# Latent attention with post-norm and a linear layer on one core: rotary parts sent through DRAM, first tables made on chip, output terms and pair order changed

## The reference

```python
HID, H, QLR, KVLR, DN, DR, DV = 512, 16, 384, 128, 128, 64, 128
cos, sin = rope_tables(s, DR)
cq = rms_norm(x @ w_qa.T, q_a_ln_w)                      # s x 384
q = (cq @ w_qb.T).reshape(b, s, H, DN + DR)
q_nope, q_pe = q[..., :DN], q[..., DN:]
q_pe = q_pe * cos + rotate_half(q_pe) * sin
ckv = x @ w_kva.T
k_pe = rotated(ckv[..., KVLR:])                          # one for all heads
kv = (rms_norm(ckv[..., :KVLR], kv_a_ln_w) @ w_kvb.T).reshape(b, s, H, DN + DV)
scores = (q_nope . k_nope + q_pe . k_pe) * (DN + DR) ** -0.5, causal
out = softmax(scores) @ v
x = layernorm(x + out @ w_o.T)
x = layernorm(x + x @ (weight * scale_weight[:, None]).T + bias)
```

## Time and profile before

| | us |
|---|---|
| median of 3 runs (lowest, highest) | 1889.14 (1888.12, 1890.75) |
| the profiled execution, its own time | 1888.21 |
| its span in the trace | 1886.5 |
| prepare phase, to TensorE's first instruction of attention | 176.4 |
| linear phase, from TensorE's first instruction | 1792.9 to 1886.5 |
| TensorE busy, share of the span | 1725.7, 91% |
| mean granted TensorE clock, share of full | 0.974 |

### The profile page before, as it was taken

One profiled execution on the slowest core, in us unless ns is written; L12 is line 12 of the kernel. 1 busy time (PEld: TensorE's weight loads), 2 busy tenths in 40 slices (PEclk: granted clock), 3 DMA queues, 4 the chain that ended last, 5 costly groups with the idle time before them and its releaser, 6 DMA issues. The chain is left out here.

```text
span 1886.5 us, 28030 instructions
## 1 busy us (share of the span) xinstructions
PE 1725.7 (91%) x8729; PEld 1396.3 (74%) x8729; DVE 1393.6 (74%) x2503; ACT 1096.9 (58%) x2092; POOL 971.9 (52%) x883
## 2 busy tenths in 40 slices
PE   5995699999999999999988899999999999998586
PEld 4564578888888888888877688888887887886442
DVE  1552368888888888878766588888888888888366
ACT  2553256666676666657545566666666766666220
POOL 2320135555555555556543455565555665556455
PEclk9997899999999999999989899999999999999889
DMA  7876212121211311112121221212112111100321
GB/s 231 305 304 211 64 49 62 46 68 40 92 50 57 98 60 52 61 51 84 57 67 34 94 75 36 67 39 96 49 53 101 42 48 35 52 31 31 123 73 56
DMA packets 90138, 152.99 MB, mean 81 GB/s; under 512 B 17872, under 2 KB 60368, under 8 KB 87632
## 3 DMA queue, kind: packets, MB, share of 16 engines
q1 hardware_dynamic: 81168, 103.60, 17.5%
q0 software_dynamic: 7104, 23.60, 3.8%
q10 hardware_dynamic: 1728, 24.12, 3.0%
HBM read 87.30 MB, written 51.38 MB: 74 GB/s over the span
## 5 line engine op out<-in xcount | busy, mean ns | idle before, releaser
L1320 POOL TENSOR_TENSOR split_p<-pool,split_p 128x512 fp32r<-128x512 f32 x544 | 702.9, 1294 | 542.3 <-ACT split_p L1265 541.9
L1143 PE MATMUL rows<-q_c,key_c 128*128 128x512 f32 x1632 | 478.9, 402 | 27.9 <-issue 15.9
L1253 ACT COPY pool<-rows 128x512 f32<-128x512 f32 x480 | 281.8, 587 | 266.7 <-PE rows L1143 264.7
L1397 DVE TENSOR_TENSOR top<-rows,top 128x512 f32<-128x512 f32 x420 | 289.0, 688 | 146.6 <-ACT pool L1253 143.5
L1412 DVE TENSOR_TENSOR pool<-bank,pool 128x512 f32<-128x512 f32 x544 | 370.1, 680 | 27.0 <-PE bank L1161 27.0
L1258 ACT ACTIVATE pool<-pool 128x512 f32<-128x512 f32 x544 | 345.9, 636 | 18.8 <-DVE pool L1412 18.3
L1265 ACT CAST split_p<-pool 128x512 fp32r<-128x512 f32 x544 | 333.2, 612 | 25.0 <-PE bank L1174 25.0
L1143 PEld LDWEIGHTS rows<-q_c,key_c 128*128 128x128 f32 x1632 | 290.4, 190 | 76.2 <-issue 27.1
L1143 PE MATMUL rows<-q_pe,key_pe 128*128 128x512 f32 x1088 | 339.1, 393 | 0.0
L1424 DVE TENSOR_TENSOR bank<-bank,pool 128x512 f32<-128x512 f32 x480 | 331.1, 690 | 0.1
L1143 PEld LDWEIGHTS rows<-q_pe,key_pe 128*128 128x128 f32 x1088 | 205.7, 189 | 45.6
(11 more groups left out here) (159 smaller groups left out, 2058.8 us busy)
## 6 DMA issues: line engine op xcount, KB each, us to landing
cq<-cq_dram SPq DMA_DIRECT2D x28, 768.0 KB, 5.0
y<-y_dram SPq DMA_DIRECT2D x64, 256.0 KB, 3.0
y_dram<-y SPq DMA_DIRECT2D x64, 256.0 KB, 2.0
wq_dram<-wq ACTq DMA_DIRECT2D x4, 2304.0 KB, 11.5
wo_dram<-wo ACTq DMA_DIRECT2D x4, 2048.0 KB, 10.6
q_pe<-by_sin SPq DMA_DIRECT2D x256, 32.0 KB, 1.8
q_pe<-by_cos SPq DMA_DIRECT2D x256, 32.0 KB, 1.8
table<-table_dram SPq DMA_DIRECT2D x31, 256.0 KB, 2.9
```

Source lines behind the costliest of these rows:

```text
L1143: mm = pe.matmul(by_head(out), k, q, start=(z == 0), stop=(z == 4))
L1253: nc.scalar.copy(slot(n), SCORES[n % N_SCORES]).then_inc(scores_copied, 1)
L1320: nc.gpsimd.tensor_tensor(split_p[:, n % 2, 1, :], slot(n), stored(split_p[:, n % 2, 0, :]), ALU.subtract).then_inc(p_lo, 1)
L1397: nc.vector.tensor_tensor(out, SCORES[n % N_SCORES], slot(number(it, 0)) if t == 1 else out, ALU.max).then_inc(scores_maxed, 1)
```

## The change

The diff, cut to what acts; planner lines that only rename steps are left out.

```diff
@@ memory @@
+        self.turned_tables = self.pool[:, 0:8 * P].rearrange("p (w n) -> p w n", n=P)
+        self.table_dram = nc.dram_tensor("table_dram", (4, P, 8, P), F32, kind="Internal").ap()
+        self.pe_dram = nc.dram_tensor("pe_dram", (G * NT // 2, 2, 2, P, 2 * P), F32, kind="Internal").ap()
@@ prepare_phase, sync @@
-            sp.wait_ge(table_copied, 1)
-            for q in range(4):
-                for h in range(HG):
-                    sp.dma_start(m.table_dram[...], tables[...]).then_inc(m.table_stored, 16)
@@ prepare_phase, scalar and vector @@
-            nc.scalar.copy(tables[:, 0:2 * NCH, :], turned_tables()[:, 0:2 * NCH, :]).then_inc(table_copied, 1)
-            act.wait_ge(table_copied, 1)
-            for h in range(HG):
-                nc.scalar.copy(*first_table(h, 0)).then_inc(table_first, 1)
+            nc.scalar.copy(m.turned_tables, turned_tables()).then_inc(m.table_copied, 1)
-            dve.wait_ge(table_copied, 1)
-            for h in range(HG):
-                nc.vector.tensor_copy(*first_table(h, 1)).then_inc(table_first, 1)
@@ order @@
-PAIR_ORDER = [[0, 7, 1, 6, 2, 5, 3, 4], [4, 3, 5, 2, 6, 1, 7, 0], [0, 7, 1, 6, 2, 5, 3, 4], [4, 7, 3, 6, 2, 5, 1, 0]]
+PAIR_ORDER = [[0, 7, 1, 6, 2, 5, 3, 4]] * 3 + [[4, 7, 3, 6, 2, 5, 1, 0]]
@@ timetable @@
-            at = window_slot(s, j)
+            at = window_slot(s, j) if s or use[0] == "pe" else -1
             if use[0] == "pe":
-                yield at + 3, READ, ("round_pe", s + 2)
-                yield max(at + 4, FIRST[2 * s + 2] if s >= 0 else 0), READ, ("move_pe", s + 2)
+                late = 1 if s == -1 else 3
+                yield at + late, READ, ("round_pe", s + 2)
+                yield at + late + 1, READ, ("store_pe", s + 2)
+                yield max(at + late + 2, FIRST[2 * s + 2] if s >= 0 else at + 5), READ, ("load_pe", s + 2)
@@ attention_phase, sync @@
-                if o % NT == NT - 1 and o + 1 < N_ITER:
-                    sp.dma_start(words(m.wo), m.wo_dram[group(o)]).then_inc(wo_loaded, 16)
+            def next_wo(o):
+                sp.wait_ge(y_ready, o + 1)
+                sp.dma_start(words(m.wo), m.wo_dram[group(o)]).then_inc(wo_loaded, 16)
+            def store_tables():
+                for q in (2, 3, 0, 1):
+                    sp.dma_start(m.table_dram[q].rearrange("(h d) w n -> d h (w n)", h=HG),
+                                 m.turned_tables[HALF * q:HALF * q + HALF] ... .broadcast_to([HALF, HG, 8 * P])
+                                 ).then_inc(m.table_stored, 16)
             def load_table(s):
+                for e in range(2):      # one transfer a query tile, 128 KB each
...
-            def move_pe(s):             # 16 transfers SBUF to SBUF, then load_table(s + 2)
+            def store_pe(s):
                 for x, (part, ready) in enumerate(((by_sin, rope_hi), (by_cos, rope_lo))):
                     sp.wait_ge(ready, s + 1)
+                    sp.dma_start(m.pe_dram[s, x].rearrange("e p n -> p e n"), stored(part[:, :, :])
+                                 ).then_inc(pe_stored, 16)
+            def load_pe(s):
+                at = pair_slot(s)
+                sp.wait_ge(pe_stored, 32 * (s + 1))
+                if s:
+                    sp.wait_ge(pe_loaded, 64 * s)
+                if s >= 2:
+                    sp.wait_ge(scores_ready, finished(2 * s - 3))
+                for x in range(2):
+                    for e in range(2):
+                        row = DR * x + HALF * e
+                        sp.dma_start(stored(q_pe[row:row + HALF, :, at:at + 2 * P]),
+                                     m.pe_dram[s, x, e].rearrange("(h d) n -> d h n", h=HG)).then_inc(pe_loaded, 16)
+                if s == 1:
+                    store_tables()
+                if s == 2:
+                    sp.wait_ge(m.table_stored, 64)
+                if MADE <= s + 2 < N_PAIR:     # MADE = 4
                     load_table(s + 2)
             sp.wait_ge(m.wo_free, 16 * (NCH + 1))
             sp.wait_ge(m.cq_free, 16 * (NCH + 1))
             sp.wait_ge(y_stored, 16)
+            load_tokens(1)
             load_y(0)
-            load_tokens(1)
-            sp.wait_ge(m.table_stored, 256)
-            load_table(1)
+                elif what == "y" and at[0] % NT == NT - 1 and at[0] + 1 < N_ITER:
+                    next_wo(*at)
@@ attention_phase, tensor @@
-                        pe.wait_ge(pe_moved, 16 * MOVES * (it // 2 + 1))     # ahead of scores
                 for z, (k, q) in enumerate(terms):
+                    if z == 3 and t == 0 and it % 2 == 0:
+                        pe.wait_ge(pe_loaded, 64 * (it // 2 + 1))
...
-                pe.wait_ge(o_lo, it + 1)
-                for h in range(HG):
-                    for a, b in ((0, 0), (0, 1), (1, 0)):
+                pe.wait_ge(o_hi, it + 1)
+                terms = [(0, 0, h) for h in range(HG)] + [(0, 1, h) for h in range(HG)] + [(1, 0, h) for h in range(HG)]
+                for n, (a, b, h) in enumerate(terms):
+                    if n == 2 * HG:
+                        pe.wait_ge(o_lo, it + 1)
...
-            pe.wait_ge(mask_copied, 1)       # moved: ahead of the first spread_max
@@ attention_phase, vector @@
+            def make_table(s):               # 8 copies of 32x256 from turned_tables
+                for h in range(HG):
+                    for e in range(2):
+                        nc.vector.tensor_copy(*first_table(s, h, e)).then_inc(table_made, 1)
             def rope(s):
-                    dve.wait_ge(pe_moved, 16 * MOVES * s)
-                    dve.wait_ge(table_loaded[s % 2], 16 * ((s + 1) // 2))
+                    dve.wait_ge(pe_stored, 32 * s)
+                if s >= MADE: dve.wait_ge(table_loaded[s % 2], 32 * ((s - MADE) // 2 + 1))
+                else: dve.wait_ge(table_made, 2 * HG * (s + 1))
...
+                if s == 0:
+                    make_table(1)
+                if s + 2 < MADE:
+                    dve.wait_ge(rope_parts, 3 * (s + 1))
+                    make_table(s + 2)
...
+            make_table(0)                    # ahead of the first step
```

More of the change, by code:

```diff
@@ L201, in turned_tables @@
             return m.rows[:, 0:8 * P].rearrange("p (w n) -> p w n", n=P)
[L203 to L208, removed]
         def fill_bank(n):
@@ L743, in waits_for @@
     if what == "scores":
-        yield ("move_pe", it // 2)
+        yield ("load_pe", it // 2)
         for j in range(PAIRS):
@@ L821, in waits_for @@
         if it:
-            yield ("move_pe", it - 1)
+            yield ("store_pe", it - 1)
     elif what == "round_pe":
         yield ("rope", it)
-    elif what == "move_pe":
+    elif what == "store_pe":
         yield ("round_pe", it)
+    elif what == "load_pe":
+        yield ("store_pe", it)
         if it >= 2:
@@ L952, in attention_phase @@
         rope_lo = sem("rope_lo")
-        pe_moved = sem("pe_moved")
+        pe_stored = sem("pe_stored")
+        pe_loaded = sem("pe_loaded")
+        table_made = sem("table_made")
         table_loaded = [sem(f"table_loaded{n}") for n in range(2)]
@@ L986, in q_slot, with first_table @@
             return (it // 2 % 2) * 2 * P + tile_of(it) % 2 * P
+        def first_table(s, h, e):
+            tile = 2 * pair_of(s) + e
+            at = tile % 4 * HALF
+            return (m.table[HALF * h:HALF * h + HALF, s % 2, :].rearrange("p (w e n) -> p w e n", w=2, e=2)[:, :, e, :],
+                    m.turned_tables[at:at + HALF].rearrange("p (w g) n -> p w g n", w=2)[:, :, tile // 4, :])
         def pair_slot(s):
             return s % 2 * 2 * P
-        MOVES = 4 * HG
+        MADE = 4
         TABLE_SLOT = RING - 8
@@ new lines, in load_table @@
+            def load_table(s):
+                for e in range(2):
+                    tile = 2 * pair_of(s) + e
+                    sp.dma_start(m.table[:, s % 2, :].rearrange("p (w e n) -> p w e n", w=2, e=2)[:, :, e, :],
+                                 m.table_dram[tile % 4].rearrange("p (w g) n -> p w g n", w=2)[:, :, tile // 4, :]
+                                 ).then_inc(table_loaded[s % 2], 16)
+            def store_pe(s):
+                for x, (part, ready) in enumerate(((by_sin, rope_hi), (by_cos, rope_lo))):
+                    sp.wait_ge(ready, s + 1)
+                    sp.dma_start(m.pe_dram[s, x].rearrange("e p n -> p e n"), stored(part[:, :, :])
+                                 ).then_inc(pe_stored, 16)
@@ L1038, in move_pe @@
+            def load_pe(s):
                 at = pair_slot(s)
+                sp.wait_ge(pe_stored, 32 * (s + 1))
+                if s:
+                    sp.wait_ge(pe_loaded, 64 * s)
                 if s >= 2:
                     sp.wait_ge(scores_ready, finished(2 * s - 3))
-                for x, (part, ready) in enumerate(((by_sin, rope_hi), (by_cos, rope_lo))):
-                    sp.wait_ge(ready, s + 1)
-                    for h in range(HG):
[L1045 to L1048, removed]
@@ L1061, in _ @@
```

(30 more changed lines are left out.)

18 lines of the change are left out of this document (6 added, 12 removed).

## The result

The changed kernel takes 1812.84 us (median of 4; 1809.61 to 1813.36) against 1889.95 us beside it: ratio 0.9582, 95% interval 0.9566 to 0.9598. On the 1889.14 us of before that is 1810, or 79 us less, where 62 were forecast (1827, range 1811 to 1857). The direction was right, the size too small, and the gain lies 1 us beyond the low end of the range. The profiled execution took 1809.61 us, the shortest of the four, and its span is 1807.6 us, 78.9 less than before; the mean granted clock rose from 0.974 to 0.989.

The account below looks back on a forecast made before the run. TensorE, busy 91% of the span, was taken as the bound, so removed waits become time won. Start 28, output projection 26 and pair order 8 sum to 62 us: 1888.2 to 1826, median 1827, range 1811 to 1857.

Parts of the forecast that it names:

- part 3, the output projection: Output projection: eight matmuls going first cover TensorE's waits for the remainder, except 3.5 us near the end; minus 26 us.
- Part 1, the start: Attention's start to pair 1's scores: table stores leave the block, rotary parts go through DRAM; 28 us won, bounds 15 to 33.
- The token wait: At the start, TensorE waits 2.3 us for pair 1's tokens, loaded at 172.7 after the `cq` store lands at 167.3.
- the list of signs: Trace signs expected if right, among them attention's first instruction near 161.7 and pair 1's scores near 191.
- Part 2, the steady moves: Each pair's `q_pe` moves, 16 issues becoming six: no wait in the long windows, 0 us; at worst 3 us lost a pair.
- Part 4, the changes of group: Pair order and `wo` at the two group changes: old cost 25 us, new twice 8.5, so minus 8 us.
- The output's time did not return on other engines: Rival, output projection: the order's other engines take the time back, half of part 3 lost; 1840 us, chance 0.13.
- the start won more than the stores: Rival, attention's start: only the block's stores are won, transfers through DRAM as late as the 16 moves; 1840, chance 0.1.
- the two changes of group are not dear: Rival, group changes: a single pair 0 between long pairs costs what two cost; 1860 us, chance 0.07.
- `q_pe` is not late: Rival, each pair's first scores: `q_pe` comes late in every pair, making the kernel slower; 1920 us, chance 0.03.

Follow-up runs that it names:

- the run with four matmuls of cover: Changed kernel with the remainder's four matmuls in the middle of the twelve, so four instead of eight stand between the two waits: 1812.15 us, ratio 0.9575.
- the early wait and the two slots: Changed kernel, 16 moves inside SBUF, pair 1's queries in old slots, `q_pe` wait ahead of all five terms, pair 1's rounding and moves planned two slots later: 1819.88 us.
- the kernel with the order alone: Kernel before with only the second group's pair order changed, so the first three groups all run forward: 1879.53 us, ratio 0.9933.
- the last experiment: Changed kernel with sums' spread and output projection of the two short iterations at each group change planned three slots later: 1798.84 us, ratio 0.9503.

## Why the prediction was wrong

**The step that failed: part 3, the output projection, 26 us for a true 41.** The mechanism was right in each detail: the forecast had 29.6 us of idle less 3.5 us that stay in the last projections, and the trace of the projection alone has 29.6 less 3.2. The mistake was to take the shown idle as the price of a wait, with nothing for what a wait hides and for the low clock after it. One projection of the kernel before, start and duration:

```profile
375.30 0.39 PE L1174 MATMUL bank<-split_p,val 128*128 128x512 f32 x1
376.22 3.00 PE L1203 MATMUL rows<-wo,o_t 128*128 128x512 f32 x12 [0.54 <-POOL o_t L1325]
379.06 0.84 PE L1143 MATMUL rows<-q_c,key_c 128*128 128x512 f32 x3
```

and the same one in the kernel with the projection alone changed:

```profile
373.30 0.39 PE L1174 MATMUL bank<-split_p,val 128*128 128x512 f32 x1
373.52 2.88 PE L1204 MATMUL rows<-wo,o_t 128*128 128x512 f32 x12
376.24 0.84 PE L1143 MATMUL rows<-q_c,key_c 128*128 128x512 f32 x3
```

From the matmul before the projection to the work behind it there are 3.76 and 2.94 us: the wait cost 0.82 us and shows as 0.54. Two things are hidden. A 128x512 matmul is drawn 0.39 us long while the next one starts 0.23 us after it, so the first 0.17 us of a wait lie under the drawn end (376.22 - 375.30 = 0.92 against 0.22). And the twelve matmuls take 2.84 us to the next work instead of 2.72 after a wait. The low clock shows at the end of attention, in the last projection of all, before and with the projection alone changed:

```profile
1777.31 4.59 PE L1203 MATMUL rows<-wo,o_t 128*128 128x512 f32 x12 [2.19 <-POOL o_t L1325]
...
1737.67 2.97 PE L1204 MATMUL rows<-wo,o_t 128*128 128x512 f32 x12 [0.86 <-ACT o_t L1283]
```

Both kernels run the same 8729 matmuls in the same order, so the gaps from start to start can be compared one by one. From attention's first matmul to its last they differ by 41 us:

| where | us |
|---|---|
| idle that the trace shows (29.6 less 3.2) | 26.4 |
| idle under the drawn end of the matmul before | 6.6 |
| the projections' matmuls after a wait, at full clock, 41 times 0.1 | 4.1 |
| two projections near the end, partly at half clock before | 3.0 |
| everywhere else | 1.4 |

The run with the old wait and the new order of terms shows that it is the wait and nothing in the order, and the run with four matmuls of cover that an overlap of 0.9 us is enough.

**Part 1, the start: 28 forecast, about 24 came.** Attention's start and the idle for `q_pe` of pair 1 (3.5 forecast, 3.2 shown) were right. The token wait was 5.5 us, not 2.3: the store of `cq` took 9.5 us to land, not the 7.9 of the earlier trace rows, and ended 169.8; its successor, the tokens' load, was followed by TensorE 5.9 us later. The forecast had called its 7.9 us "rather late than early", because the table stores shared the queues. It is the other way round: the store lands in 7.9 us in the four kernels that issue 16 stores behind it and in 9.5 in the ten that don't. The run with stores back in the block, which differs from the changed kernel in nothing else, has (first line; the changed kernel second)

```profile
DMA to landing us min/median/max: 7.9/7.9/7.9
...
DMA to landing us min/median/max: 9.5/9.5/9.5
```

Why is open. One more term was put at nothing: VectorE's first masked tile comes behind eight table copies that end at 185.4 and two additions, and TensorE waits 1.2 us for it. And the first scores of pair 1 start at 191.2, as the list of signs says ("near 191"), by luck: the forecast's terms put these scores at 187.5 and only its 3.5 us of wait behind them. The stores in the block are worth 9 to 11 us, not 14.7, since the wait for tokens takes up the rest; the six transfers and the early queries are worth nothing each, and together with the early wait and the two slots 6 to 7 us.

**Part 2, the steady moves: 0, confirmed.** Sixteen moves a pair are as good as six transfers in the kernel's time. The DMA rows of the changed kernel (compare):

```profile
q_pe<-pe_dram SPq DMA_DIRECT2D x128, 128.0 KB, 2.7
...
pe_dram<-by_sin SPq DMA_DIRECT2D x32, 256.0 KB, 2.1
pe_dram<-by_cos SPq DMA_DIRECT2D x32, 256.0 KB, 2.2
...
wo<-wo_dram SPq DMA_DIRECT2D x3, 2048.0 KB, 8.7
```

The stores to DRAM land in 2.1 to 2.2 us in the median and the loads in 2.7, as estimated (2.0 and 2.8). At the start, with tokens on the way, the four stores of the first two pairs took 5.5 to 6.2 us. The Trainium skill's page (DMA: Bandwidth & Descriptors, anatomy of one DMA, which describes transfers issued by GpSimd, while SyncE issues these) warns of a long delay when the write goes to HBM. In the medians no such surplus shows: 256 KB written to DRAM land 0.5 us sooner than 128 KB read from it.

**Part 4, the changes of group: 8 forecast, 9.5 to 12.7 came.** The step is right, with one error inside. `wo` was to be waited for 3.5 us, since it is issued 1 us earlier; the waits are 4.4 and 4.3 us. In the changed kernel's timeline

```profile
612.50 0.33 SPq L1008 DMA_DIRECT2D wo<-wo_dram  x1
...
621.39 4.18 PE L1226 MATMUL rows<-wo,o_t 128*128 128x512 f32 x9 [4.36 <-issue]
```

the load is issued as VectorE's addition starts (612.5), yet lands in 8.7 us instead of 7.9: a load and a store of `y` and two stores of rotary parts follow within 5 us. With the rotary parts moved inside SBUF again it lands in 8.0, and the waits are 3.6 and 3.5 us, the forecast's number: the earlier issue does win (4.7 and 5.2 us in the kernel with the order alone), and the stores through DRAM take 0.8 us of it back each time. The output-bank wait at a single pair 0 was 0.3 us instead of 2. That a change of group costs more than its shown waits is seen in the last experiment: 8.7 us of waits went, and 10 to 14 us with them, and the low clock behind the wait went too.

**The end** was not in the forecast at all. The linear phase waits 14.15 us where it was 11.04, in every kernel with the new projection (13.8 to 14.4) and in none with the old (11.0 to 12.8). GpSimd's last remainder and the loads that follow it, in the changed kernel,

```profile
1697.67 1.29 POOL L1347 TENSOR_TENSOR o_t<-o_sum,o_t 128x512 fp32r<-128x512 f32 x1 [2.56 <-ACT o_t L1305]
...
1700.42 5.31 POOL L1369 DMA_DIRECT2D pool<-y_dram  x10
```

and before:

```profile
1775.91 1.26 POOL L1325 TENSOR_TENSOR o_t<-o_sum,o_t 128x512 fp32r<-128x512 f32 x1 [3.90 <-ACT o_t L1283]
...
1778.64 5.31 POOL L1347 DMA_DIRECT2D pool<-y_dram  x10
```

The last projection no longer waits for that remainder, and TensorE ends at 1700.7 where it ended at 1781.9; the ten issues end 5.0 us after it where they ended 2.0 us after. The linear phase begins 9.1 us after the last of them, before 9.0: they hold the block open, so 3 of the last microseconds won are given back.

**Rivals.** The output's time did not return on other engines, the start won more than the stores, the two changes of group are not dear, and `q_pe` is not late: all four fell. The missing case was the one above the forecast. Nor does the low end of the range follow from the parts: part 4 gives 25 us as the most that it can win, the sum takes 15. With the 25 it would have been 1801, and the result inside.

## What to carry to other kernels

On an engine whose instructions overlap, read a wait from start to start, against the same pair of instructions undisturbed: here the true cost was 0.82 us for 0.54 us shown, and 41 us for 26 in all, 3 of them low clock. Where a product of several terms waits for the last-made operand, put the terms that don't need it first; four matmuls of 0.23 us covered 1.3 us of GpSimd, of which TensorE had waited 0.7 in most places. And undo edits together as well as singly before calling one useless: two that were worth nothing alone held 6 to 7 us, together with two others.

## What was not expected of the hardware

- A 256 KB store of SBUF to DRAM (2.1 us) is about as fast as the 32 KB moves inside SBUF (1.8 us), so two large stores and four loads replace 16 moves (10.2 us of issue) at no loss, and here at no gain.
- The landing of a 2 MB load rose from 7.9 to 8.7 us when four smaller transfers were issued behind it on the same queue; without the two stores among them it was 8.0.
- A 1.5 MB store landed in 7.9 us with 16 stores of another queue issued behind it, and in 9.5 us without them.
- One matmul group after a wait of half a us took 0.12 us more than without, at full granted clock.
